# Attention over edges in a graph kernel: the products that only clear accumulators go, and one output projection serves two items

## The reference, cut to what matters

```
Q = (h @ Wq).reshape(n, H, D)          # H = 4 heads, D = 64
K = (h @ Wk).reshape(n, H, D)
V = (h @ Wv).reshape(n, H, D)
score = einsum('ehd,ehd->eh', Q[src], K[dst]) / sqrt(D)
attn = softmax(score, axis=1)          # over the heads of an edge
m = V[src] * attn[:, :, None]
h_new = segment_sum(m, dst, num_segments=n)
h_proj = h_new.reshape(n, H * D) @ Wo
...
x = x + layernorm(h_proj + h)
```

## Time and profile before

| | |
|---|---|
| median of 3 runs | 4016.44 us (4012.95 to 4023.06) |
| profiled execution | 4015.06 us |
| its span, from first to last instruction | 4013.3 us |
| granted TensorE clock over the span | 0.689 of full speed |
| the loop of `attend`, 232 to 1664 us of the span | 1432 us for 98 items |
| TensorE, VectorE, ScalarE, GpSimd busy in that stretch | 691, 988, 658, 752 us |

### The profile page before, as it was taken

The page is one execution under the profiler, slowest core; times in us unless marked ns, Lnnn a source line. Parts: engine busy times, 40 slices in busy tenths (PEclk is TensorE's granted clock), DMA queues, the critical chain, the costliest instruction groups (busy, mean ns, idle before and its releaser), DMA issues. The chain is left out here.

```text
span 4013.3 us, 59848 instructions
## 1 busy us (share of the span) xinstructions
PE 1849.8 (46%) x16923; PEld 1321.5 (33%) x16923; DVE 2235.3 (56%) x4872; ACT 1211.0 (30%) x3818; POOL 1590.9 (40%) x1665
## 2 busy tenths in 40 slices
PE   6744444444444444431312227852111356655377
PEld 5633333333333333221101116751111355545222
DVE  7776666676666666531301003341111599997899
ACT  1154444444444444321001002200000133334644
POOL 1055555555555555546766660016667200000000
PEclk8866666666666666665655559975555688896599
DMA  7711122111111111352222220024443222221000
GB/s 247 292 40 40 40 40 41 41 41 38 40 40 40 40 41 41 103 194 52 59 53 53 53 49 1 1 62 132 127 112 80 70 75 81 79 75 41 0 0 8
DMA packets 399308, 267.12 MB, mean 67 GB/s; under 512 B 321456, under 2 KB 349293, under 8 KB 399073
## 3 DMA queue, kind: packets, MB, share of 16 engines
q1 hardware_dynamic: 306278, 87.81, 10.2%
q10 hardware_dynamic: 41472, 118.96, 8.2%
q0 software_dynamic: 51488, 59.40, 6.1%
HBM read 158.59 MB, written 107.47 MB: 66 GB/s over the span
## 5 line engine op out<-in xcount | busy, mean ns | idle before, releaser
L1231 POOL DMA_INDIRECT sorted_edges<-r_load,r_to x800 | 793.6, 992 | 666.1 <-DMA r_to<-places 389.5
L804 POOL DMA_INDIRECT hsrc<-h,edges x808 | 775.5, 960 | 704.0 <-PE ps L997 470.6
L872 DVE TENSOR_TENSOR prod<-ps,hsrc 125x1024 f32<-125x1024 f32 x200 | 244.9, 1225 | 334.2 <-remote 190.1
L1409 PE MATMUL ps<-R,w_work 128*128 128x64 bf16 x3000 | 152.1, 206 | 342.2 <-issue 194.7
L995 PE MATMUL ps<-blank 128*64 128x160 bf16 x101 | 31.5, 312 | 602.7 <-remote 596.5
L1748 DVE TENSOR_TENSOR w_work<-ps,w_work 128x384 f32<-128x384 f32 (+1 forms) x160 | 91.1, 570 | 352.1 <-remote 349.4
L1546 ACT ACTIVATE R<-w_work 128x384 bf16<-128x384 f32 (+1 forms) x160 | 85.8, 536 | 662.2 <-DVE w_work L1748 619.2
L1409 PEld LDWEIGHTS ps<-R,w_work 128*128 128x128 bf16 x3000 | 124.3, 106 | 379.7 <-issue 210.5
L951 ACT ACTIVATE lo<-ramp,edges 125x128 bf16<-125x128 int16 x808 | 246.8, 388 | 0.0
L863 DVE TENSOR_SCALAR hot<-ramp,small 125x400 bf16<-125x400 int16 x800 | 218.6, 325 | 47.9 <-issue 46.1
L961 ACT ACTIVATE prod<-prod 125x64 f32<-125x64 f32 x800 | 194.2, 244 | 152.3 <-DVE prod L872 150.8
(11 more groups left out here) (414 smaller groups left out, 4277.0 us busy)
## 6 DMA issues: line engine op xcount, KB each, us to landing
w_work<-sorted_edges ACTq DMA_DIRECT2D x42, 1000.0 KB
r_load<-in_edge_attr_dram SPq DMA_DIRECT2D x80, 312.5 KB
dstrow<-dst_rows SPq DMA_DIRECT2D x101, 234.4 KB
sorted_edges<-A ACTq DMA_DIRECT2D x10, 2000.0 KB, 9.8
A<-counts SPq DMA_DIRECT2D x12, 1600.0 KB
counts<-A ACTq DMA_DIRECT2D x4, 4000.0 KB, 33.7
sorted_edges<-A ACTq DMA_DIRECT2D x15, 1000.0 KB, 9.6
hsrc<-h,edges POOLq DMA_INDIRECT x808
```

Of the source, the lines that this page charges most:

```text
L804: g.indirect_dma_start(out=hsrc[:, s, t, :], out_offset=None, in_=S.h0[:, :], in_offset=bass.IndirectOffsetOnAxis(ap=edges.bitcast(I32)[:, ...
L872: v.tensor_tensor(prod[0:TP, :].rearrange("p (t h f) -> p t h f", t=HT, h=H), S.ps[0:TP, hf * 1024:(hf + 1) * 1024].rearrange("p (t h f) - ...
L1231: g.indirect_dma_start(out=S.sorted, out_offset=bass.IndirectOffsetOnAxis(ap=to[:, hf, t:t + 1], axis=0), in_=load[:, hf, t, :], in_offset ...
L1409: mm = pe.matmul(acc[:, GROUPS[n][0] + b, :], lo[:, k, b, :], mp[:, k, b, d, :], start=False, stop=False, skip_group_check=True)
```

## The change

Five edits, all in `attend`:

1. The products with `blank` go (L995 and L1035). The first real product of each bank has `start=True` in their place; for the second count bank that is the first tile that reaches it. `blank` shrinks to two columns.
2. `project` runs once for two items, at the end of the s = 1 item, with `U` now holding two slots and four products of 2 x 39 columns in place of four of 40 for each item. After the loop one more handles the last slot alone.
3. VectorE adds nothing to `hpw` in the s = 0 item and two windows in the s = 1 item, the second after the first has been waited for.
4. All of it works on 39 columns of the 40 (`SEEN`); the second addition of counts is 19 x 25 in place of 20 x 25.
5. `bring_sums` still waits for `u` and then `proj`, but `proj` now counts rounds: the two values differ (`n + 1` and `j + 1`).

```diff
-    blank = sb("blank", [P, 512], BF16)
-    U = sb("U", [D, H * W], F32)
+    blank = sb("blank", [P, 2], BF16)
+    U = sb("U", [D, 2, H * W], F32)
+    SEEN = OFF[-1] + SUB
+    FIRST = (0, next(t for t in range(T) if OFF[t] * NB + SK > HK))
...
-                    v.wait_ge(q["proj"], i + 2)
-                    v.tensor_tensor(S.hpw[:, bass.ds(before, W)], S.hpw[:, bass.ds(before, W)], S.ps[0:D, 3584:3584 + W],
-                                    ALU.add).then_inc(q["proj_free"], 1)
+                    if s == 1:
+                        v.wait_ge(q["proj"], j + 2)
+                        own.step(v.tensor_tensor(S.hpw[:, bass.ds(before, SEEN)], S.hpw[:, bass.ds(before, SEEN)],
+                                                 S.ps[0:D, 3584:3584 + SEEN], ALU.add))
+                        v.tensor_tensor(S.hpw[:, bass.ds(b0, SEEN)], S.hpw[:, bass.ds(b0, SEEN)],
+                                        S.ps[0:D, 3584 + W:3584 + W + SEEN], ALU.add).then_inc(q["proj_free"], 1)
...
-            def bring_sums(n):
+            def bring_sums(n, j, s):
                 act.wait_ge(q["u"], n + 1)
-                act.wait_ge(q["proj"], n + 1)
-                act.copy(U[:, :], S.ps[0:D, 3072:3072 + H * W]).then_inc(q["u_free"], 1)
+                act.wait_ge(q["proj"], j + 1)
+                act.copy(U[:, s, :].rearrange("d (h w) -> d h w", h=H)[:, :, 0:SEEN],
+                         S.ps[0:D, 3072:3072 + H * W].rearrange("d (h w) -> d h w", h=H)[:, :, 0:SEEN]).then_inc(q["u_free"], 1)
...
-                pe.matmul(sums, blank[:, 0:D], blank[:, 0:H * W], start=True, stop=False, skip_group_check=True)
                 for t in range(T):
                     mm = pe.matmul(sums.rearrange("d (h w) -> d h w", h=H)[:, :, OFF[t]:OFF[t] + SUB], hsrc[0:TP, s, t, :],
-                                   AO[0:TP, t, :, :], start=False, stop=(t == T - 1), skip_group_check=True)
+                                   AO[0:TP, t, :, :], start=(t == 0), stop=(t == T - 1), skip_group_check=True)
...
+                to = S.ps[0:D, 3584:3584 + c * W].rearrange("d (s w) -> d s w", s=c)[:, :, 0:SEEN]
                 for h in range(H):
-                    mm = pe.matmul(S.ps[0:D, 3584:3584 + W], S.Mo[:, h * D:(h + 1) * D], U[:, h * W:(h + 1) * W],
+                    mm = pe.matmul(to, S.Mo[:, h * D:(h + 1) * D], U[:, 0:c, h * W:h * W + SEEN],
                                    start=(h == 0), stop=(h == H - 1))
...
-                    for k in range(2):
-                        pe.matmul(S.ps[:, 2048 + 512 * k:2048 + 512 * k + HK], blank[:, 0:P], blank[:, 0:HK],
-                                  start=True, stop=False, skip_group_check=True)
...
-                    project(i)
+                    if s == 1:
+                        project(j, 2)
             weigh(n * 2, 1)
-            project(n * 2)
+            project(n, 1)
```

More of the change, by code:

```diff
@@ L744, in attend @@
     third1, third2 = 32000, 64000
+    SEEN = OFF[-1] + SUB
+    FIRST = (0, next(t for t in range(T) if OFF[t] * NB + SK > HK))
+    assert OFF[0] == 0 and all(OFF[t + 1] <= OFF[t] + SUB for t in range(T - 1)) and W // 2 < SEEN < W and OFF[FIRST[1]] <= W // 2
     def pairs_of(eng):
@@ L853, in _ @@
                     i = j * 2 + s
-                    own = Own(v, q["own"], j * (2 * STEPS + 1) + s * STEPS + 5)
+                    own = Own(v, q["own"], j * (2 * STEPS + 2) + s * STEPS + 5)
                     th = "p (t h) -> p t h"
@@ L883, in add_counts @@
                     def add_counts(k):
-                        part = S.Apad[:, 0:NB * NP].rearrange("p (b n) -> p b n", b=NB)[:, :, bass.ds(b + k * (W // 2), W // 2)]
-                        seen = S.ps[:, 2048 + 512 * k:2048 + 512 * k + HK].rearrange("p (w b) -> p b w", b=NB)
+                        w = W // 2 if k == 0 else SEEN - W // 2
+                        part = S.Apad[:, 0:NB * NP].rearrange("p (b n) -> p b n", b=NB)[:, :, bass.ds(b + k * (W // 2), w)]
+                        seen = S.ps[:, 2048 + 512 * k:2048 + 512 * k + w * NB].rearrange("p (w b) -> p b w", b=NB)
                         v.tensor_tensor(part, part, seen, ALU.add).then_inc(q["count_free"], 1)
@@ L901, in _ @@
                     else:
-                        before = b0
                         own.step(v.tensor_copy(last[:, :], spot[0:1, s, 1:2]))
@@ L925, in _ @@
                                     a4.unsqueeze(3).to_broadcast([TP, T, H, SUB]), ALU.mult).then_inc(q["ao"], 1)
-                    assert own.n == STEPS + s, (own.n, s)
+                    assert own.n == STEPS + 2 * s, (own.n, s)
             n = pairs_of(v)
             b = v.value_load(last[0:1, 0:1], min_val=0, max_val=LASTB)
-            v.wait_ge(q["proj"], n * 2 + 2)
-            v.tensor_tensor(S.hpw[:, bass.ds(b, W)], S.hpw[:, bass.ds(b, W)], S.ps[0:D, 3584:3584 + W], ALU.add)
+            v.wait_ge(q["proj"], n + 2)
+            v.tensor_tensor(S.hpw[:, bass.ds(b, SEEN)], S.hpw[:, bass.ds(b, SEEN)], S.ps[0:D, 3584:3584 + SEEN], ALU.add)
         @block.scalar
@@ L970, in _ @@
                     i = j * 2 + s
-                    bring_sums(i)
+                    bring_sums(i, j, s)
                     add(i, 0)
@@ L976, in _ @@
                     rows(i + 1, 1 - s, j * 16 + 16 + 16 * s)
-            bring_sums(pairs_of(act) * 2)
+            n = pairs_of(act)
+            bring_sums(n * 2, n, 0)
         @block.tensor
@@ L1001, in weigh, with project @@
                 pe.sem_inc(q["u"], 1)
-            def project(n):
-                pe.wait_ge(q["u_free"], n + 2)
-                pe.wait_ge(q["proj_free"], n + 1)
+            def project(j, c):
+                pe.wait_ge(q["u_free"], j * 2 + c + 1)
+                pe.wait_ge(q["proj_free"], j + 1)
                 pe.sem_inc(q["carrier"], 1)
+                to = S.ps[0:D, 3584:3584 + c * W].rearrange("d (s w) -> d s w", s=c)[:, :, 0:SEEN]
                 for h in range(H):
-                    mm = pe.matmul(S.ps[0:D, 3584:3584 + W], S.Mo[:, h * D:(h + 1) * D], U[:, h * W:(h + 1) * W],
+                    mm = pe.matmul(to, S.Mo[:, h * D:(h + 1) * D], U[:, 0:c, h * W:h * W + SEEN],
                                    start=(h == 0), stop=(h == H - 1))
@@ L1044, in _ @@
                                 mm = pe.matmul(S.ps[:, at0 + c0:at0 + c1], lo[0:TP, s, t, :], hot[0:TP, t, c0 - k0:c1 - k0],
-                                               start=False, stop=False, skip_group_check=True)
+                                               start=(t == FIRST[k]), stop=False, skip_group_check=True)
                         mm.then_inc(q["hot_free"], 1)
```

## The result

The changed kernel took 3902.71 us (median of 4 runs, 3882.3 to 3911.47), the kernel before on the same chip 4018.91 (median of 4, 4012.95 to 4023.06): a ratio of 0.9714, 95% interval 0.9691 to 0.9737. That ratio holds for some chips only. In the runs that follow the kernel before took 4012 and 4038 us on two chips, and 2861, 2858 and 2857 us on three others; on one of these three the changed kernel was run as well (e5), and there it is 0.8% **slower**. On the chips where the kernel before takes about 4000 us, completions are seen microseconds late while a train of gathers runs. I call this the hold, the first kind of chip "with the hold" and the second "without". Each chip was met at one time only, so the runs don't show whether it is the chip itself or something around it.

What follows compares the result with a forecast made beforehand. The prediction took a ring of `weigh` and gathers, with a wait going by the gather, as the bound. Its terms, -10.1 us and four zeros, gave 4004.96 us profiled, 4006 as a median; range 4000 to 4072.

Steps and rivals of the forecast that it cites:

- The ring: Pace of an item in the loop: 2.81 us from `weigh` to first gather, then 11.79 us to the next `weigh`.
- They count 0: The counts' two clearing products, 0.99 us as recorded, end long before the counts are needed, so removing them gains 0.
- The cover is again: The projection's change counts 0, hidden under 5.55 to 6.21 us of waiting before `weigh`; without cover up to 15 us.
- The clearing product of `weigh`: In the ring, 0.10 us before the first fp32 product, 101 times: removing it gains 10.1 us.
- saves nothing: Rival: without `weigh`'s clearing product the first fp32 product's weight load is exposed, so no gain, 4016 us; chance 0.06.
- VectorE's addition: Moved from s = 0 to s = 1, before `AO`: covered by 4.60 us, so 0; without cover 10 us.
- The table load: ScalarE's load before the copy in s = 0, 1.29 us later, lies within the gather: 0; at most 64.5 us.
- More is gained: Rival: fewer completions during the gather shorten the wait before `weigh`, 10 us more, 3996 us; chance 0.06.
- From one first gather to the next `weigh` still 11.8 us: Sign in the loop's timeline that the forecast is right: this stretch of the item keeps its length.

Runs made afterwards that it cites:

- e5: The changed kernel, as it is, on a chip without the hold: 2880.44 us, ratio 1.0079 to the kernel before.
- e8: The kernel before, unchanged, run again for its trace on a chip with the hold: 4019.94 us (one run).
- e9: The changed kernel with eight products that nobody reads added in the s = 0 item, with the hold: 3993.53 us, ratio 0.9953 to the kernel before.
- e17: The kernel before without clearing products, a projection for every item, table load early, with the hold: 4024.33 us, ratio 0.9974.
- e3: The kernel before without clearing products, a projection for each item, table load early, without the hold: 2864.01 us, ratio 1.0015.
- e14: The kernel before, unchanged, run for its trace on a chip without the hold: 2856.22 us.
- e11: The same kernel as e3, on another chip without the hold: 2862.25 us, ratio 1.0009 to the kernel before.
- e1: The changed kernel with the two waits before the copy of the sums swapped, so the table load is early, without the hold: 2869.07 us, ratio 1.0030.
- e10: The changed kernel with the table load early, as e1, on a chip with the hold: 3900.01 us (one run).
- e6: The changed kernel with the table load early, as e1, on another chip without the hold: 2868.86 us, ratio 1.0041 to the kernel before.
- e2: The kernel before with only the table load moved behind the wait for the sums, without the hold: 2868.45 us, ratio 1.0029.
- e7: The same kernel as e2, on another chip without the hold: 2865.10 us, ratio 1.0024 to the kernel before.
- e16: The changed kernel with four products that nobody reads added in the s = 0 item, with the hold: 3963.42 us, ratio 0.9834 to the kernel before.

## Why the prediction was wrong

**What bounds the kernel.** The ring over `weigh` and the first gather, and that the wait goes by the gather, are right for a held item. "A completion of TensorE that falls into the later part of a gather is seen by others only at its end" is the sentence that failed, in its "only": it depends on how many instructions TensorE has in the item. The two items that I compared both had 28 + 26 products and loads, and I took as a law of time what was a matter of number. "At its end" was loose as well: the two places read for it have the held completion 1.95 us and 0.15 us behind the last gather's end, and e8 has it before that end.

**The projection, and the clearing products of the counts: "They count 0", "The cover is again" the wait in front of `weigh`.** This is the term that was wrong. In the s = 0 item I hid 20 products and loads fewer (28 + 26 against 18 + 16) behind a wait that existed only because of their number. The whole change is worth 115 us with the hold, and nearly all of it stands in this term that I had at 0: e9 gives eight products back and loses 93 us. The clearing products alone (e17) bring 0.26%, in an interval that holds nothing as well. The other part alone, a projection for two with the clearing products kept, was not run, so how the gain divides between the two parts is not shown.

**The clearing product of `weigh`, -10.1 us.** Its front is as forecast. Without the hold `weigh`'s fp32 products follow `AO` by 0.15 us (changed kernel and e3) where it was 0.25 (e14), the 0.10 of the earlier trace rows. But the products then take 0.03 longer to the first gather (2.73 from the first fp32 product, in place of 2.70), which was the rival "saves nothing" by a third. With the hold e17 is 0.26% faster, 10.5 us, interval a loss of 1.6 to a gain of 23: it fits and doesn't prove. Without the hold it is worth nothing, since VectorE sets the pace: e3 and e11 have a pair in 21.64 and 21.65 us, e14 in 21.61, and e3 is 0.15% slower than the kernel before.

**VectorE's addition, 0.** With the hold it is covered, as said. Without it, it costs. Take the projection for two (e1) against a projection for each (e3), on the same chip and both with the load early: a pair takes 21.83 us against 21.64, 9 us over the loop of the traces (5 us between the medians of the runs). In the s = 1 item two additions with a wait between them now stand in front of `AO`, which starts 1.01 us behind the second addition of counts where it was 0.69, and the item is 0.31 us longer (10.92 against 10.61). In the s = 0 item that stretch is as long as before (0.68 against 0.69), though the item is 0.12 us shorter. The estimate was 0.4 more and 0.2 less.

**The table load, 0, with up to 64.5 as the great risk.** With the hold it is 0, as forecast: e10 3900.01, the changed kernel 3902.71 (another chip, one run against four). The reason is only partly mine: its 1.29 us are lost in the s = 0 item (11.4 against 10.0 us) and come back in the s = 1 item, whose gather can't start before the first has ended. Without the hold it costs 11.6 us in the changed kernel (e5 against e6), a fifth of the full price, and 7.0 and 7.4 in the kernel before (e2, e7). ScalarE is late there anyway: the copy follows `weigh`'s first product by 2.72 us in e6 with the load early and by 3.42 with it late, 0.7 and not 1.29 more.

**The rivals.** "More is gained: fewer completions in the gather's time let the rest through sooner" was the right one, with a chance of 0.06, 10 us where it was 115, and a true "no row speaks for it". None of the rivals held that the wait in front of `weigh` could be missing on another chip, as it is in e14.

**What would show it.** "From one first gather to the next `weigh` still 11.8 us": true in the s = 1 items, 8.68 (1514.86 to 1523.54) in the others. That line showed the failure at once.

## What to carry to other kernels

When a wait has no engine behind it and no row explains it, its length is not a cover to hide work under: ask what changes the wait itself, and vary the number of instructions, not only their time. Run the kernel before on several chips before a per cent is worth arguing over. Here one and the same change is 2.9% faster on a chip with the hold and 0.8% slower on one without, and the version with the table load early (e6, e10) keeps the gain with the hold and loses only 0.4% without; where there is no hold, none of the versions that ran is faster than the kernel before.

## What the runs showed of the hardware

With the hold, the steps of SyncE, the engine that issues these transfers, come later as well. In the kernel before, one item's transfers with the hold, and then without it (e14):

```profile
1523.83 0.36 SPq L760 DMA_DIRECT2D spot<-items  x1
1524.92 0.02 SPq L763 DMA_DIRECT2D edges<-edge_table  x1
1527.08 0.70 SPq L776 DMA_DIRECT2D rwin<-r  x1
1529.93 0.70 SPq L769 DMA_DIRECT2D dstrow<-dst_rows  x1
```

```profile
880.67 0.36 SPq L760 DMA_DIRECT2D spot<-items  x1
...
881.33 0.30 SPq L763 DMA_DIRECT2D edges<-edge_table  x1
...
881.83 0.33 SPq L776 DMA_DIRECT2D rwin<-r  x1
...
882.46 0.34 SPq L769 DMA_DIRECT2D dstrow<-dst_rows  x1
```

The four take 1.8 us from first to last without the hold and 6.1 with it (medians of 97 items 1.78 and 5.98). The last of them waits for `there`, which ends 1.1 us behind the start of the first in either trace, so that isn't the reason. The lateness comes in steps: in e16 the held s = 0 items start `weigh` 1.1, 1.8, 2.5 or 3.2 us behind `AO`, 0.7 us apart, as long as two of SyncE's rows. VectorE's `hot` in the changed kernel stood 2.94 us for no reason that the trace names while the gather ran. Only the stages with GpSimd's indirect transfers have it (808 of them in `attend`, 801 in `spread`, none in the others): `front`, `mlp` and `gat` take 192, 142 and 216 us on either kind of chip, `attend` 1494 against 1119, `spread` 1969 against 1186.

The traces show one more thing that goes with the hold: with it, most records of semaphore changes are missing. The kernel before has 59848 instructions in either trace, but 15983 such records with the hold and 46583 without (e14). `front`, `mlp` and `gat` have the same number in both to within 2; `attend` has 5805 against 23391, `spread` 7889 against 20902. All eight traces with the hold have 15562 to 17412, all eleven without 46288 to 46796. What the profile says ended a wait is worked out from these records, so with the hold the names of the releasers ("remote", "issue") stand on about a quarter of them in `attend`; the starts and ends that the readings above rest on don't need them.

What the hold is stays open. Late steps on several engines, a limit by number, and records that go missing in just these stages would fit a buffer that fills with something each instruction leaves behind and that drains badly while the gathers run. One such thing would be the records of the profile: every run here, the timed ones too, has a span and a granted clock in its result, so all were recorded. The Trainium skill, "NOTIFIC — Programmer's Manual", section "2.4 When the ring fills", gives three answers of a full queue of records: by default the new record is lost, or the oldest is overwritten, or the engine blocks until there is room. The traces agree with lost records, by the counts above; that an engine blocks for want of room is not shown by any run here, nor whether there is a hold in a run that isn't recorded.
